# Expert biases spread over the partitions and added by VectorE, the adjacency fetched one stage later

## What is computed

```python
y = o.transpose(0, 2, 1, 3).reshape(b, n, d) @ Wo
gate = jax.nn.softmax(y @ gate_W + gate_b, axis=-1)              # 8 weights a node
hid = jax.nn.gelu(jnp.einsum('bnd,edf->bnef', y, W1) + b1)       # 8 experts, 512 -> 256
eo = jnp.einsum('bnef,efd->bned', hid, W2) + b2                  # 256 -> 512
out = jnp.einsum('bned,bne->bnd', eo, gate)                      # x = x + out
# layer 1, graph part: neigh = adjacency @ layernorm(x), then products with W_self and W_neigh
```

## Time and profile before

| | before |
|---|---|
| median of 3 runs (lowest to highest) | 1569.64 us (1569.23 to 1570.88) |
| the profiled execution | 1569.58 us |
| its span, first to last instruction | 1567.8 us |
| `graph_in` and `graph_causal` | 0 to 540 us |
| `experts` | 540 to 882.8 us |
| `graph_last` | 882.8 to 1018 us |
| `top_layer` | 1018 us to the end |
| PE, DVE, ACT, POOL busy over the span | 93%, 61%, 46%, 39% |
| mean granted TensorE clock (1 is 2.4 GHz) | 0.981 |

### The profile page before, as it was taken

One profiled execution on the slowest core, in us unless ns is written; L12 is line 12 of the kernel. 1 busy time (PEld: TensorE's weight loads), 2 busy tenths in 40 slices (PEclk: granted clock), 3 DMA queues, 4 the chain that ended last, 5 costly groups with the idle time before them and its releaser, 6 DMA issues. The chain is left out here.

```text
span 1567.8 us, 22143 instructions
## 1 busy us (share of the span) xinstructions
PE 1451.7 (93%) x8144; PEld 898.9 (57%) x8144; DVE 963.7 (61%) x1779; ACT 721.3 (46%) x1406; POOL 611.4 (39%) x502
## 2 busy tenths in 40 slices
PE   5888999999898899999999899889999988997998
PEld 3554545447777654454556544546676776775664
DVE  7998254326666411123123323768999999999994
ACT  5542114336666410110111230256777887888783
POOL 4887200040645200000000060017786785785863
PEclk8999999999999989999999999989999999999999
DMA  7001000054242240000000200003020110101001
GB/s 249 1 2 85 0 0 1 0 145 101 52 77 52 75 179 0 0 1 0 0 0 1 81 0 0 1 17 78 10 58 3 35 30 5 35 11 25 1 1 66
DMA packets 37915, 58.04 MB, mean 37 GB/s; under 512 B 17056, under 2 KB 21796, under 8 KB 37552
## 3 DMA queue, kind: packets, MB, share of 16 engines
q1 hardware_dynamic: 36496, 54.05, 12.9%
q10 hardware_dynamic: 1312, 2.56, 0.4%
HBM read 31.06 MB, written 5.87 MB: 24 GB/s over the span
## 5 line engine op out<-in xcount | busy, mean ns | idle before, releaser
L1525 POOL TENSOR_TENSOR tl_ex<-tl_ex,tl_left 128x1250 f32<-128x1250 f32 x80 | 209.7, 2621 | 28.9 <-ACT tl_left L1860 24.2
L1344 DVE SCALAR_TENSOR_TENSOR X<-ex_ps_x,g,X 128x512 f32<-128x512 f32 x80 | 59.9, 751 | 192.6 <-PE ex_ps_x L1237 192.6
L1665 PE MATMUL tl_banks<-identf,tl_ex 128*128 128x128 f32 x800 | 134.4, 283 | 23.6 <-ACT tl_pt L1881 14.0
L2029 POOL TENSOR_TENSOR lo<-xn,hi 128x512 f16<-128x512 f32 x5 | 5.9, 1186 | 373.0 <-ACT hi L2133 373.0
L1881 ACT COPY tl_pt<-tl_banks 128x512 f32<-128x512 f32 (+1 forms) x200 | 108.1, 541 | 91.2 <-PE tl_banks L1665 90.7
L1210 PE MATMUL ex_ps_h<-yt,w 128*128 128x512 f32 (+1 forms) x384 | 144.5, 530 | 0.0
L1237 PE MATMUL ex_ps_x<-w,hid 128*128 128x512 f32 (+1 forms) x320 | 143.1, 599 | 0.0
L1290 ACT ACTIVATE hid<-ex_ps_h,b 128x512 f32<-128x512 f32 (+1 forms) x48 | 29.1, 608 | 242.6 <-PE ex_ps_h L1210 242.6
L1665 PEld LDWEIGHTS tl_banks<-identf,tl_ex 128*128 128x128 f32 x800 | 89.0, 141 | 84.9 <-issue 44.4
L1951 DVE MAX8 tl_m<-tl_banks 128x8 f32<-128x1250 f32 x80 | 116.3, 1453 | 10.1 <-PE tl_banks L1635 9.9
L1957 DVE MAX8 tl_m<-tl_left 128x8 f32<-128x1250 f32 x80 | 117.1, 1464 | 2.8
(11 more groups left out here) (283 smaller groups left out, 2952.4 us busy)
## 6 DMA issues: line engine op xcount, KB each, us to landing
tl_kl<-tl_KT SPq DMA_DIRECT2D x16, 320.0 KB, 4.4
tl_qs<-tl_QO SPq DMA_DIRECT2D x16, 320.0 KB, 5.7
kl<-KT SPq DMA_DIRECT2D x14, 320.0 KB, 4.2
qs<-QO SPq DMA_DIRECT2D x14, 320.0 KB, 5.8
w<-in_L_ffn_W SPq DMA_DIRECT2D x8, 512.0 KB
w<-in_L_ffn_W SPq DMA_DIRECT2D x4, 1024.0 KB, 8.9
at_kept<-AT SPq DMA_DIRECT2D x1, 3200.0 KB, 9.0
AT<-at_kept SPq DMA_DIRECT2D x1, 3200.0 KB, 18.7
```

Of the source, the lines that this page charges most:

```text
L1525: pool.tensor_tensor(ex[:, n % EXS, 0:N], ex[:, n % EXS, 0:N], left[:, n % LEFT, :], ALU.subtract).then_inc(s_probs, 1)
L1665: mm = pe.transpose(ps_t[:, b * P:(b + 1) * P], ex[:, n % EXS, a + b * P:a + (b + 1) * P], m.identf[:, :])
```

## The change

The second biases are fetched as a broadcast, [128, 8, 512], so that each partition holds all eight rows (2 MB in SBUF, where the adjacency lay), and the gate bias as [128, 8]. VectorE adds the gate bias ahead of the softmax, and for each expert and tile adds gate times bias with one scalar_tensor_tensor from SBUF (80 in all, `add_bias`). A list `steps` says what VectorE does at each expert: expert 0 its product alone, expert 1 its product and biases 0 and 1, experts 2 to 5 their own, expert 6 also bias 7, expert 7 its product alone. The K=1 products, the gate transposes, the copies `gt`, the K=8 products and their additions go. The adjacency is fetched by the first instruction of `graph_last`'s SP queue, and the first gather waits for it. The addition of a tile waits for the last update of that tile, whichever kind it was.

```diff
-        for t in tiles(G):
-            x_use["b2", t] = len(x_use)
+    steps = [[("ps", 0)], [("ps", 1), ("b2", 0), ("b2", 1)]] + [[("ps", e), ("b2", e)] for e in range(2, EX - 1)]
+    steps[-1].append(("b2", EX - 1))
+    steps.append([("ps", EX - 1)])
...
-            sp.dma_start(AT[:, :, :].rearrange("p a d -> p (a d)"), at_kept[:, :]).then_inc(s_at, 16)
+            sp.dma_start(b2[:, :, :].rearrange("p e d -> p (e d)"), io["L0_ffn_b2"].rearrange("(a e) d -> a (e d)", a=1)
+                         .broadcast_to([P, EX * D])).then_inc(s_b2, 16)
-            sp.wait_ge(s_at, 16)
...
-                        pe.matmul(to, yt[:, G % 2, k, r * P:r * P + rows(t)], gw[:, k, :], start=(k == 0), stop=False)
-                    mm = pe.matmul(to, m.ones[0:1, 0:rows(t)], gb[:, :], start=False, stop=True)
+                        mm = pe.matmul(to, yt[:, G % 2, k, r * P:r * P + rows(t)], gw[:, k, :],
+                                       start=(k == 0), stop=(k == KD - 1))
...
-
-            def gate_turn(G):
-                pe.wait_ge(s_gate, G + 1)
-                for r, t in enumerate(tiles(G)):
-                    mm = pe.transpose(ps_g[0:EX, r * P:r * P + rows(t)], g[0:rows(t), t, :],
-                                      m.identf[0:rows(t), 0:rows(t)])
-                mm.then_inc(s_gate_t, 1)
-
-            def add_b2(G):
-                pe.wait_ge(s_gate_row, G + 1)
-                for r, t in enumerate(tiles(G)):
-                    v = x_use["b2", t]
-                    open_x(v)
-                    pe.matmul(x_bank(v)[0:rows(t), :], gt[:, r * P:r * P + rows(t)], b2[:, :], start=True, stop=True
-                              ).then_inc(s_x_ps, 1)
 
...
-                        if G:
-                            w2_of(G - 1, EX - 1)
-                        gate_turn(G)
-                    else:
-                        if e == 1:
-                            add_b2(G)
+                    if e:
                         w2_of(G, e - 1)
+                    elif G:
+                        w2_of(G - 1, EX - 1)
...
-                dve.tensor_reduce(most, lg, AX_X, ALU.max).then_inc(s_step, 1)
-                dve.wait_ge(s_step, 3 * G + 1)
-                dve.tensor_tensor(gx[:, 0, 0:nr, :], lg, most.unsqueeze(2).broadcast_to([P, nr, EX]), ALU.subtract
-                                  ).then_inc(s_shifted, 1)
+                dve.tensor_tensor(gx[:, 0, 0:nr, :], lg, gb[:, :].unsqueeze(1).broadcast_to([P, nr, EX]), ALU.add
+                                  ).then_inc(s_step, 1)
+                dve.wait_ge(s_step, 4 * G + 1)
+                dve.tensor_reduce(most, gx[:, 0, 0:nr, :], AX_X, ALU.max).then_inc(s_step, 1)
+                dve.wait_ge(s_step, 4 * G + 2)
+                dve.tensor_tensor(gx[:, 0, 0:nr, :], gx[:, 0, 0:nr, :], most.unsqueeze(2).broadcast_to([P, nr, EX]),
+                                  ALU.subtract).then_inc(s_shifted, 1)
...
-            def gate_rows(G):
-                w = GROUPS[G][1]
-                dve.wait_ge(s_gate_t, G + 1)
-                if G:
-                    dve.wait_ge(s_x_ps, x_use["b2", tiles(G - 1)[-1]] + 1)
-                dve.tensor_copy(gt[:, 0:w], ps_g[0:EX, 0:w]).then_inc(s_gate_row, 1)
+            last = {}
 
             def add(G, e):
+                if e == 0:
+                    dve.wait_ge(s_gate, G + 1)
                 for t in tiles(G):
                     n = rows(t)
                     x_t = m.X[0:n, t, :]
                     v = x_use[e, t]
                     dve.wait_ge(s_x_ps, v + 1)
-                    if e == "b2":
-                        dve.tensor_tensor(x_t, x_t, x_bank(v)[0:n, :], ALU.add).then_inc(s_x_free, 1)
-                    else:
-                        dve.wait_ge(s_x_free, v - len(tiles(G)) + 1)
-                        dve.scalar_tensor_tensor(out=x_t, in0=x_bank(v)[0:n, :], scalar=g[0:n, t, e:e + 1], in1=x_t,
-                                                 op0=ALU.mult, op1=ALU.add).then_inc(s_x_free, 1)
-
+                    if t in last:
+                        dve.wait_ge(*last[t])
+                    dve.scalar_tensor_tensor(out=x_t, in0=x_bank(v)[0:n, :], scalar=g[0:n, t, e:e + 1], in1=x_t,
+                                             op0=ALU.mult, op1=ALU.add).then_inc(s_x_free, 1)
+                    last[t] = (s_x_free, v + 1)
+
+            def add_bias(G, e):
+                dve.wait_ge(s_b2, 16)
+                for t in tiles(G):
+                    n = rows(t)
+                    x_t = m.X[0:n, t, :]
+                    dve.wait_ge(*last[t])
+                    dve.scalar_tensor_tensor(out=x_t, in0=b2[0:n, e, :], scalar=g[0:n, t, e:e + 1], in1=x_t,
+                                             op0=ALU.mult, op1=ALU.add).then_inc(s_biased, 1)
+                    last[t] = (s_biased, EX * tiles(G)[0] + len(tiles(G)) * e + t - tiles(G)[0] + 1)
+
+            gates(0)
             for G in range(NG):
-                if G == 0:
-                    gates(0)
-                gate_rows(G)
-                add(G, "b2")
                 for e in range(EX):
-                    add(G, e)
+                    for kind, f in steps[e]:
+                        (add if kind == "ps" else add_bias)(G, f)
                     if e == 5 and G + 1 < NG:
                         gates(G + 1)
-                dve.wait_ge(s_x_free, x_use[EX - 1, tiles(G)[-1]] + 1)
                 for t in tiles(G):
+                    dve.wait_ge(*last[t])
                     dve.bn_stats(m.stats[:, t, :], m.X[:, t, :])
...
+            sp.dma_start(m.AT[:, :, :].rearrange("p a d -> p (a d)"), at_kept[:, :]).then_inc(s_at, 16)
             for dst, src in ahead[1]:
...
+                            pe.wait_ge(s_at, 16)
                     for t in range(NT):
...
-            gb = space("gb", 136320, [1, EX])
+            gb = space("gb", 136320, [P, EX])
-            b2 = space("b2", 136416, [EX, D])
+            b2 = space("b2", 102400, [P, EX, D])
...
```

More of the change, by code:

```diff
@@ L1105, in _, with experts @@
                     keep_o(pair_of[n - LAG - 1])
-def experts(nc, m, io, space, QO, wo, gw, gb, b1, b2, s_early, early_done, w1, w2, AT, at_kept, ahead):
+def experts(nc, m, io, space, QO, wo, gw, gb, b1, s_early, early_done, w1, w2, b2, ahead):
     GROUPS = pieces(N)
@@ L1138, in experts @@
                 x_use[e, t] = len(x_use)
+    steps = [[("ps", 0)], [("ps", 1), ("b2", 0), ("b2", 1)]] + [[("ps", e), ("b2", e)] for e in range(2, EX - 1)]
+    steps[-1].append(("b2", EX - 1))
+    steps.append([("ps", EX - 1)])
     with ExitStack() as ctx:
         s = Stage(nc, m, ctx, "ex")
-        (s_at, s_w2, s_h_ps, s_h_free, s_logits, s_shifted, s_expd, s_step, s_gate, s_gate_t, s_gate_row,
-         s_x_ps, s_x_free, s_w2_read) = s.signals(
-            "at w2 h_ps h_free logits shifted expd step gate gate_t gate_row x_ps x_free w2_read")
+        (s_b2, s_w2, s_h_ps, s_h_free, s_logits, s_shifted, s_expd, s_step, s_gate, s_x_ps, s_x_free, s_biased
+         ) = s.signals("b2 w2 h_ps h_free logits shifted expd step gate x_ps x_free biased")
         yt = space("yt", 61440, [P, 2, KD, BANK])
@@ L1149, in experts @@
         gs = space("gs", 147392, [P, 3, NT])
-        gt = space("gt", 147520, [EX, BANK])
         ps_h = s.psum("ps_h", [P, HB, BANK])
@@ L1194, in logits @@
                 if G:
-                    pe.wait_ge(s_gate_row, G)
+                    pe.wait_ge(s_gate, G)
                 for r, t in enumerate(tiles(G)):
@@ L1250, in _ @@
                             own(G + 1, e - 2)
-                    if e == 0:
-                        if G:
-                            w2_of(G - 1, EX - 1)
-                        gate_turn(G)
-                    else:
-                        if e == 1:
-                            add_b2(G)
+                    if e:
                         w2_of(G, e - 1)
+                    elif G:
+                        w2_of(G - 1, EX - 1)
                     if e == 6 and G + 1 < NG:
@@ L1314, in gates @@
                 dve.wait_ge(s_logits, G + 1)
-                dve.tensor_reduce(most, lg, AX_X, ALU.max).then_inc(s_step, 1)
-                dve.wait_ge(s_step, 3 * G + 1)
-                dve.tensor_tensor(gx[:, 0, 0:nr, :], lg, most.unsqueeze(2).broadcast_to([P, nr, EX]), ALU.subtract
-                                  ).then_inc(s_shifted, 1)
+                dve.tensor_tensor(gx[:, 0, 0:nr, :], lg, gb[:, :].unsqueeze(1).broadcast_to([P, nr, EX]), ALU.add
[5 more added lines that the diff above has]
+                                  ALU.subtract).then_inc(s_shifted, 1)
                 dve.wait_ge(s_expd, G + 1)
                 dve.tensor_reduce(total, gx[:, 1, 0:nr, :], AX_X, ALU.add).then_inc(s_step, 1)
-                dve.wait_ge(s_step, 3 * G + 2)
+                dve.wait_ge(s_step, 4 * G + 3)
                 dve.reciprocal(inv, total).then_inc(s_step, 1)
-                dve.wait_ge(s_step, 3 * G + 3)
+                dve.wait_ge(s_step, 4 * G + 4)
```

(26 more changed lines are left out.)

## The result

| | before | after |
|---|---|---|
| median of 4 runs (lowest to highest) | 1569.92 us (1569.23 to 1570.88) | 1547.15 us (1546.69 to 1548.86) |
| the profiled execution, its span | 1569.58, 1567.8 us | 1547.18, 1545.4 us |
| before `experts` (0 to its first product) | 540.2 us | 543.0 us |
| `experts`, to the barrier | 342.7 us | 319.6 us |
| from there to the last transpose of `graph_last` | 133.3 us | 131.6 us |

A forecast was written before the change was run, and what follows sets the result against it. TensorE, busy 339.2 of 342.8 us, was taken to bound the experts' stage. 1569.6 - 14.0 (removed products) - 3.4 (clock) + 0.7 (tail) = 1552.9 us, range 1549 to 1558.

The forecast's parts named there:

- What bounds the stage: Experts' stage: TensorE, busy 339.2 of 342.8 us, bounds it, so a removed TensorE instruction moves everything behind it.
- The gate bias: Logits on TensorE: removing the K=1 pairs saves 0.31 us a tile, 3.1 us over ten tiles.
- Transposes and second biases: TensorE in the three groups: removing gate transposes saves 1.1 us, removing the K=8 second-bias products 9.8 us.
- The tail: End of the experts' stage: biases ahead of VectorE's last additions make the end 0.7 us later.
- The clock: Half-clock stretches in the experts' stage: one goes and the first shortens, 1.7 us each, 3.4 us gained.
- The bounds: Limits set on the forecast: clock gain from 0 to 6.8 us, whole time from 1549 to 1558 us.
- "clock gives more" rival: Experts' stage: half-clock stretches after the later logits go or halve too; 1549.5 us, 18% chance.
- VectorE: Experts' stage: 80 added biases, 0.68 us apart, never make TensorE wait; tightest at the second group's end, 1.1 us spare.
- That rival: VectorE's bias instructions from two float32 SBUF tensors take 1.5 us each; 1568 or 1565 us, 4% chance.
- Transfers: Adjacency fetched at the next stage's head and 2 MB bias broadcast both land in time: zero cost, 28 and 13 us cover.
- the bound of 45: Worst price for landing the 2 MB bias broadcast: eight 256 KB broadcasts of 5.6 us one after another, 45 us.
- Later stages: Half-clock stretches after the experts' stage shift against the work: 1.7 us either way, no sign.

The follow-up runs named there:

- K made 128: Kernel before, with its K=1 and K=8 products given 128 rows, the added rows zero; ratios 0.9957 and 0.9943 in two measurements.
- Tail moved: Changed kernel, with the last group's biases 5 to 7 added beside experts 4 and 5; 1546.6 us, ratio 0.9837.
- the four traces of the changed order: Changed kernel, its unchanged repeat, its adjacency fetched last in the queue, its last group's biases moved earlier; ratios 0.9846, 0.9855, 0.9848, 0.9837.
- second-biases-only trace: Changed kernel with the gate bias's K=1 products put back on TensorE; 1557.7 us, ratio 0.9906 against the kernel before.

## Why the prediction was wrong

The direction and the bound were right. The stage's gain of 23.1 us in the profiled executions is 14.6 of products and tail and 8.5 of clock; I had 14.0 - 0.7 = 13.3 and 3.4. So 1.3 us are missing in the first and 5.1 in the second, and the second alone put the result outside the range. Both come from the same kind of error, reading a cost only where the removed instruction stands.

- **What bounds the stage.** Right. TensorE stays busy, and the stage moves with it one for one.
- **The gate bias: 3.1 us forecast, 3.7 to 4.0 measured.** The 3.7 is the stage at full clock, the 4.0 TensorE's order of time. This step failed, too, by its size: the price of 0.31 us a tile, from the pair's start to the next tile's, holds only the change back to 128 rows. The change to one row is paid ahead of the pair's start: the earlier trace rows has eight products in 0.99 us, and they take 0.87 to 0.90 where no pair stands among them; in the second group the first eight, with no pair ahead of them, take 0.88 us before (672.24 to 673.12) and 0.81 with K made 128 (670.78 to 671.59).
- **Transposes and second biases: 1.1 + 9.8 forecast, 10.9 together with the tail measured**, so 11.3 without it. By TensorE's order of time the second group lost 4.16 us (706.52 to 717.55 before, less the 6.87 of its 16 hidden products) and the third 2.65, against 4.17 and 2.5.
- **The tail: +0.7 forecast, +0.4 measured.** Tail moved shows that it is the biases there.
- **The clock: 3.4 us forecast with a bound of 6.8, about 7 to 8.5 measured.** This is the step that failed and broke the range. I took the stretch behind the bias products away and shortened the first, and left those behind the later logits "since the logits stay". In the profiled execution they were gone, and the first was shorter by 6.8 us of half-clock time, where I had 3.4: 17.0 us of half-clock time went, 8.5 us. By the four traces of the changed order against the two of before it is 22.1 - 7.7 = 14.4 us, 7.2 us. Of these 14.4 us of half-clock time some 2.5 lay behind the first logits (I had 3.4), 5.1 behind the later ones (I had none) and 6.8 behind the bias products (I had 3.4, from the only trace that I had; the second trace has three stretches there). I had read each stretch as the property of a line. But the logits alone are a third shorter (5.1 to 3.5 us at full clock for four tiles), and so measured, the second group's have a stretch in two of six traces instead of all three, and the third group's in none of six instead of all three. Logits doubled bring all back. That the profiled executions differ by 17.0 us and not by 14.4 is chance.
- **The bounds.** The "clock gives more" rival was right in kind, at 18%; its time of 1549.5 still left the first stretch at most of its length, and had the low product price. 14.6 + 8.5 = 23.1 us is the stage's measured gain. On the median, 22.8 us, scatter has a part: the two measurements of the ratio are 0.9846 and 0.9855. The range ended at 1549 because it gave the clock 6.8 us at most.
- **VectorE.** Right in detail. 80 biases at 743 ns, eight in 5.38 us, and the first addition behind them starts at 807.02; TensorE does not wait there. The rule of the Trainium skill in "Vector Engine (DVE) Microarchitecture Reference", section "Points that are easy to get wrong", that two SBUF sources which are not bf16 halve this instruction's throughput, does not show here: 743 ns from SBUF, 750 ns with one source in PSUM. That rival is refuted.
- **Transfers.** Right. The adjacency landed after 10.8 us with 45 us to its use, and the 2 MB broadcast after 16.2 us, a third of the bound of 45. The first gather product follows the last own product without a gap.
- **Later stages.** 1.7 us either way was too narrow for the single profile: the part ahead of the stage alone ranged over 5.3 us in thirteen traces, on unchanged work.

What stays open: why the same order of products has 3.4 us at half clock in one execution and 13.7 in another, and whether K=1 or the added time carries the stretches behind the logits in the second-biases-only trace. The runs show that both few rows (8, with 512 columns) and a longer run of few columns (8, with 128 rows) can bring one, not how they add. Each kernel but the one before, the changed one and K made 128 has a single trace.

## What to carry to other kernels

Where a stage is bound by TensorE, price a block of small products by the distance between the starts of its full-size neighbours, with and without the block; its own rows miss what it costs the products around it. Then look at the granted clock behind each run of thin products (few columns or few rows) and count it into the price: here 50 removed instructions gave 15 us of their own and about 7 more of clock. If thin products must stay, try them in shorter runs between dense blocks: the first logits, 1.8 us at a time, had no half clock in two traces, where the whole 3.6 us had it in five of five.

## What the runs showed of the hardware

- A change of the number of rows between neighbouring products (128 to 1 and back) costs about 0.09 us each way: 1.30 against 1.12 us for the same ten instructions of 8 columns, once with a pair of one row and once with all rows 128.
- The clock fell to half while TensorE was recorded as busy without a gap, behind products of 8 columns or of 8 rows (five of nine blocks), and behind none of six of the same blocks of 512 columns once they had 128 rows, the added ones zero.
- Executions differ by up to 5 us in the clock alone: four traces of the same order of products have 3.4 to 13.7 us at half clock in one stage, while the stage at full clock repeats to 0.1 us in the three that have the same tail.
